# Attention's first near terms stored in two interleaved halves, later ones in two pieces

## The reference

```
x = x + 0.5 * L0_ffn(layernorm(x))          # switch MoE, 8 experts
x = x + L0_attn(layernorm(x))               # the part that is changed
x = x + 0.5 * L0_ffn(layernorm(x))
x = x + 0.5 * L1_ffn(layernorm(x))
x = x + L1_attn(layernorm(x))
x = x + 0.5 * L1_ffn(layernorm(x))
```

```
pos_k  = rel_embeddings @ Wk + bk                       # by head
scores = q k^T / scale
c2p    = take(q pos_k^T, clip(rel + 32, 0, 63))         # by (q, k)
p2c    = take(k pos_k^T, clip(-rel + 32, 0, 63))^T
probs  = softmax(scores + (c2p + p2c) / scale)
out    = layernorm((probs v) Wo + bo + hidden)
```

## Time and profile before

| | us |
|---|---|
| median of 3 runs | 788.8 (788.06 to 790.25) |
| the profiled execution | 788.52 |
| its span in the trace | 786.8 |
| attention's first instruction | 116.6 |
| the first `add_terms` | 180.16 |

### The profile page before, as it was taken

The page is one execution under the profiler, slowest core; times in us unless marked ns, Lnnn a source line. Parts: engine busy times, 40 slices in busy tenths (PEclk is TensorE's granted clock), DMA queues, the critical chain, the costliest instruction groups (busy, mean ns, idle before and its releaser), DMA issues. The chain is left out here.

```text
span 786.8 us, 16609 instructions
## 1 busy us (share of the span) xinstructions
PE 583.0 (74%) x5220; PEld 417.2 (53%) x5220; DVE 531.2 (68%) x1878; ACT 437.1 (56%) x944; POOL 219.6 (28%) x274
## 2 busy tenths in 40 slices
PE   4499927727999999999999998343993661686660
PEld 3387923324666566667666666233982451364460
DVE  7612235815787678989999995771226888766887
ACT  2034524415888788888888884631551523464522
POOL 1743422000950391095040000056442100212000
PEclk9999977866999999999999998655997655799655
DMA  8669525989989899999954413725552000000001
GB/s 251 179 182 391 185 79 169 289 342 269 283 274 335 220 278 348 324 225 271 338 157 129 124 48 99 165 76 146 180 166 71 0 1 1 0 1 2 0 1 53
DMA packets 133602, 130.79 MB, mean 166 GB/s; under 512 B 29565, under 2 KB 109485, under 8 KB 131853
## 3 DMA queue, kind: packets, MB, share of 16 engines
q1 hardware_dynamic: 126668, 103.61, 46.3%
q0 software_dynamic: 4736, 25.07, 8.7%
q10 hardware_dynamic: 2112, 1.05, 0.5%
HBM read 73.43 MB, written 52.92 MB: 161 GB/s over the span
## 5 line engine op out<-in xcount | busy, mean ns | idle before, releaser
L1442 DVE CUSTOM_DVE_ANT_0 l0am_prob<-l0am_ps_s,l0am_bias 128x512 f32<-128x512 f32 x256 | 161.6, 687 | 56.1 <-PE l0am_ps_s L1519 34.9
L1361 ACT ACTIVATE l0am_prob<-l0am_prob,l0am_neg_top 128x512 f32<-128x512 f32 x256 | 172.1, 730 | 19.1 <-DVE l0am_neg_top L1442 19.0
L1531 PE MATMUL l0am_ps_t<-c_ident,l0am_prob 128*128 128x128 f32 x1024 | 138.2, 279 | 0.0
L1531 PEld LDWEIGHTS l0am_ps_t<-c_ident,l0am_prob 128*128 128x128 f32 x1024 | 113.8, 142 | 16.7 <-issue 16.6
L1355 ACT COPY l0am_probT<-l0am_ps_t 128x512 f32<-128x512 f32 x128 | 69.0, 590 | 45.6 <-PE l0am_ps_t L1531 45.6
L1519 PE MATMUL l0am_ps_s<-l0am_ks,l0am_qs 32*128 32x512 f32 x512 | 74.0, 647 | 21.7 <-DVE l0am_neg_top L1442 19.5
L1429 DVE COPY l0am_probT<-l0am_ps_t 128x512 f32<-128x512 f32 x128 | 82.2, 683 | 2.5 <-PE l0am_ps_t L1531 2.4
L764 DVE COPY l0f_xsT<-l0f_psT 128x128 f32<-128x128 f32 x46 | 13.4, 292 | 97.5 <-PE l0f_psT L872 97.5
L593 ACT ACTIVATE l0f_h<-l0f_psU,l0f_experts 128x128 f32<-128x128 f32 x184 | 52.6, 368 | 47.2 <-PE l0f_psU L882 47.2
L1544 PE MATMUL l0am_ps_c<-l0am_probT,l0am_v 128*9 128x128 f32 x2048 | 67.9, 273 | 0.9 <-issue 0.9
L509 POOL DMA_INDIRECT token_results<-l0f_ys,l0f_token_i x46 | 44.3, 962 | 62.5 <-DVE l0f_ys L774 61.9
(11 more groups left out here) (312 smaller groups left out, 976.6 us busy)
## 6 DMA issues: line engine op xcount, KB each, us to landing
l0am_bias<-near_terms SPq DMA_DIRECT2D x128, 192.0 KB, 4.8
near_terms<-l0am_near POOLq DMA_DIRECT2D x12, 1536.0 KB, 8.3
l0f_mine<-l0f_experts SPq DMA_DIRECT2D x46, 256.0 KB, 2.8
l0am_rows_k<-position_k SPq DMA_DIRECT2D x16, 448.0 KB, 6.9
near_terms<-l0am_near SPq DMA_DIRECT2D x1, 6144.0 KB, 19.8
position_q<-l0am_rows SPq DMA_DIRECT2D x20, 224.0 KB, 4.8
position_k<-l0am_rows SPq DMA_DIRECT2D x20, 224.0 KB, 4.9
l0am_rows_q<-position_q SPq DMA_DIRECT2D x20, 224.0 KB, 6.0
```

What stands on the lines that cost most here:

```text
L1361: nc.scalar.activation(prob[:, k, :], prob[:, k, :], ACT.Exp, bias=neg_top[:, k:k + 1], scale=-1.0)\
L1442: dve.tensor_tensor_reduce(out=prob[:, k, :], in0=ps_s[:, j, :], in1=bias[:, j, at:at + S], scale=-1.0, scalar=HUGE, op0=ALU.add, op1=ALU.min,
L1531: last = pe.transpose(ps_t[:, u % 2, i, :], prob[:, u % SLOTS_, i * P:(i + 1) * P], ident[:, :])
```

## The change

There are five edits.

1. Batch 0's rows are laid out otherwise: heads 0 to 7 on the even partitions, heads 8 to 15 on the odd ones. Each of its row loads is issued as two DMAs, one a half (`half_view` steps two partitions at a time). Waits on `rows_in` count one batch more.
2. `store_first_near(half)` stores one half: 64 partitions, every second one. The even half holds groups 0 and 1. Bias loads of group 0 wait for it alone; the odd half is stored after them, and group 2's first bias load waits for it.
3. The first two row loads of batch 1 are issued between the first half's store and the wait for it; places 2 to 9 get new steps.
4. GpSimd stores the near terms of batches 1 to 3 in two DMAs of 32 queries each.
5. Batch 3's chunks are made at quads 15 to 26 (before: 13 to 24), and its row loads come at quads 24 to 33 (before: 21 to 30).

The diff, without two parts that only repeat what is listed (the k loads of batch 0, the same edit on TensorE):

```diff
@@ -116,7 +116,7 @@
 NEAR_AT = {0: 0, 3: 576, 1: 896, 2: 1344}
 BIAS_COLS = 1664
 FIRST_KEY = {t: NEAR_AT[t] - (2 * t - 1) * 64 for t in range(T4)}
-LATER_PIECES = tuple((q0, q0 + 16) for q0 in range(0, 64, 16))
+LATER_PIECES = ((0, 32), (32, 64))
 CHUNK_SPAN = CHUNK * S + MARGIN
 TAB_SPAN = MARGIN + TABLE_CHUNKS * CHUNK_SPAN
@@ -162,9 +162,9 @@
     steps = {}
-    for later, quads in ((1, [-1, -1, 0, 0, 1, 1, 2, 2, 3, 3]), (2, range(9, 19)), (3, range(21, 31))):
+    for later, first, quads in ((1, 2, [-4, -4, 0, 1, 1, 2, 2, 3]), (2, 0, range(9, 19)), (3, 0, range(24, 34))):
         for place, quad in enumerate(quads):
-            steps.setdefault(divmod(quad + T4, T4), []).append((later, place))
+            steps.setdefault(divmod(quad + T4, T4), []).append((later, first + place))
     return steps
@@ -1100,7 +1101,7 @@
         rows_out = [sem(f"rows_out{k}") for k in range(ROW_BUFS)]
         rows_in, far_out = [sem(f"rows_in{k}") for k in range(TABLE_CHUNKS)], sem("far_out")
         near_out = kept.enter_context(nc.semaphore(f"{name}_near_out"))
-        first_near_out = sem("first_near_out")
+        first_near_out = [sem(f"first_near_out{half}") for half in range(2)]
         near_steps, near_dve, near_pool = sem("near_steps"), sem("near_dve"), sem("near_pool")
         tiles_in = [sem(f"tiles_in{k}") for k in range(2)]
         bias_in = [sem(f"bias_in{t}") for t in range(T4)]
@@ -1124,16 +1125,23 @@
         def late_quad(cn):
-            return cn - EARLY + 1
+            return cn - EARLY + 1 if cn < LAST else cn - LAST + 15
+
+        late = {late_quad(cn): cn for cn in range(EARLY, B * BATCH_CHUNKS)}
         def view(what, offset, *dims):
             t = what[:, :].tensor
             return bass.AP(t, offset, [(t.shape[1], P), *dims])
+        def half_view(what, half, offset, *dims):
+
+            t = what[:, :].tensor
+            return bass.AP(t, half * t.shape[1] + offset, [(2 * t.shape[1], P // 2), *dims])
+
         def near_build(engine, b, between):
             def arrived(pair):
-                engine.wait_ge(rows_in[pair], 16 * PAIR_LOADS[pair] * (b + 1))
+                engine.wait_ge(rows_in[pair], 16 * PAIR_LOADS[pair] * (b + 2))
             arrived(0)
             arrived(1)
@@ -1176,6 +1184,12 @@
                 def load_q_rows(b, k, arrived):
                     r = k * ROWS_CHUNK
+                    if b == 0:
+                        for half in range(2):
+                            sp.dma_start(half_view(rows_q, half, r * 64, (64, ROWS_CHUNK), (1, 64)),
+                                         bass.AP(dram["tab"][0].tensor, row_address(b, r) + half * HEADS // 2 * S,
+                                                 [(64, P // 2), (HEADS * S, ROWS_CHUNK), (1, 64)])).then_inc(arrived, 16)
+                        return
                     sp.dma_start(view(rows_q, r * 64, (64, ROWS_CHUNK), (1, 64)),
                                  bass.AP(dram["tab"][0].tensor, row_address(b, r),
                                          [(64, P), (HEADS * S, ROWS_CHUNK), (1, 64)])).then_inc(arrived, 16)
...
@@ -1196,11 +1216,11 @@
                     wait_chunk(b * BATCH_CHUNKS + place)
                     (load_q_rows, load_k_rows)[side](b, CHUNK_ORDER[pair], rows_in[pair])
-                def store_first_near():
+                def store_first_near(half):
                     part = 64 * WIN
-                    own = [(part, P), (1, part)]
-                    sp.dma_start(bass.AP(dram["near"].tensor, 0, own), bass.AP(near[:, :].tensor, 0, own)).then_inc(first_near_out, 16)
+                    sp.dma_start(bass.AP(dram["near"].tensor, half * (P // 2) * part, [(part, P // 2), (1, part)]),
+                                 half_view(near, half, 0, (1, part))).then_inc(first_near_out[half], 16)
                 def store_far(b, part):
@@ -1244,11 +1264,14 @@
                         sp.wait_ge(far_out, 64)
                         load_tiles(0)
                 sp.wait_ge(near_dve, 1)
-                store_first_near()
+                store_first_near(0)
+                load_rows(1, 0)
+                load_rows(1, 1)
                 sp.wait_ge(filled, 1)
-                sp.wait_ge(first_near_out, 16)
+                sp.wait_ge(first_near_out[0], 16)
                 for t in range(T4):
                     load_bias(0, t)
+                store_first_near(1)
                 for cn in range(EARLY - ROW_BUFS, EARLY):
                     store_chunk(cn)
@@ -1266,12 +1289,13 @@
                         if n:
                             sp.wait_ge(neg_ready, 16 * (n - 1) + 4 * (t + 1))
-                            if g == 0 and t == 0:
+                            if n == GROUPS // 2 and t == 0:
+                                sp.wait_ge(first_near_out[1], 16)
+                            elif g == 0 and t == 0:
                                 sp.wait_ge(near_out, 16 * len(LATER_PIECES) * b)
                             load_bias(n, t)
-                        for cn in range(EARLY, B * BATCH_CHUNKS):
-                            if n and late_quad(cn) == 4 * (n - 1) + t:
-                                store_chunk(cn)
+                        if n and T4 * (n - 1) + t in late:
+                            store_chunk(late[T4 * (n - 1) + t])
                         for later, place in ROW_STEPS.get((n, t), ()):
                             if place == 0 and later > 1:
                                 sp.wait_ge(near_pool, later - 1)
@@ -1303,7 +1327,8 @@
                 for b in range(1, B):
                     if b == 1:
-                        pool.wait_ge(first_near_out, 16)
+                        for half in range(2):
+                            pool.wait_ge(first_near_out[half], 16)
                     near_build(pool, b, between).then_inc(near_pool, 1)
                     pool.wait_ge(near_pool, b)
                     for k, (q0, q1) in enumerate(LATER_PIECES):
@@ -1380,9 +1405,8 @@
                     if q < QUADS:
                         exp(4 * q + 2)
                         exp(4 * q + 3)
-                    cn = EARLY + q - 1
-                    if EARLY <= cn < B * BATCH_CHUNKS:
-                        copy_rows(cn, ps_g[:, :])
+                    if q in late:
+                        copy_rows(late[q], ps_g[:, :])
             @block.vector
             def _(dve):
...
```

More of the change, by code:

```diff
@@ L1074, in relative_attend @@
         EARLY = 2 * BATCH_CHUNKS
+        LAST = 3 * BATCH_CHUNKS
         stats, mv = sb("stats", [P, TILES, 6]), sb("mv", [P, TILES, 2])
@@ L1185, in load_k_rows @@
                     for n0, n1, start in NARROW_PIECES[k]:
+                        if b == 0:
+                            for half in range(2):
+                                sp.dma_start(half_view(rows_k, half, n0 * NARROW, (NARROW, n1 - n0), (1, NARROW)),
+                                             bass.AP(dram["tab"][1].tensor, row_address(b, n0) + start - 64 + half * HEADS // 2 * S,
+                                                     [(64, P // 2), (HEADS * S, n1 - n0), (1, NARROW)])).then_inc(arrived, 16)
+                            continue
                         sp.dma_start(view(rows_k, n0 * NARROW, (NARROW, n1 - n0), (1, NARROW)),
@@ L1556, in _ @@
                         score(q)
-                    cn = EARLY + q - 2
                     if 3 <= q:
-                        if EARLY <= cn < B * BATCH_CHUNKS:
-                            pe.wait_ge(rows_ready, cn + 1)
+                        if q - 1 in late:
+                            pe.wait_ge(rows_ready, late[q - 1] + 1)
                         turn_heads(q - 3)
@@ L1569, in _ @@
                         turn(4 * (q - 1) + 3)
-                    cn = EARLY + q - 1
-                    if EARLY <= cn < B * BATCH_CHUNKS:
-                        if cn == EARLY + 1:
-                            pe.wait_ge(rows_ready, cn)
+                    if q in late:
+                        if late[q] == EARLY + 1:
+                            pe.wait_ge(rows_ready, late[q])
                         if 3 <= q:
                             pe.wait_ge(heads_ready, q - 2)
-                        row_products(cn, ps_g[:, :])
+                        row_products(late[q], ps_g[:, :])
         clear_semaphores(nc, own_sems + aside.own_sems)
```

## The result

| | before | after |
|---|---|---|
| median, 20 runs each on one chip | 789.42 us | 786.58 us |
| ratio after / before, 95% interval | | 0.9962 (0.9945 to 0.9979) |
| profiled execution, its span | 788.52, 786.8 | 788.47, 786.8 |

The change gains 2.8 us by the medians, 1.7 to 4.3 by the interval. The forecast was 783, a gain of 5.6.

A forecast was written before the change was run, and what follows sets the result against it. The loop's head was taken to be bound by store, wait, load, with TensorE busy throughout the loop. Terms: -5.1 (first bias) + 2.5 (ScalarE) - 3.0 (slow quads) = -5.6, so 788.5 becomes 782.9, say 783; own range 779 to 787, whole range 779 to 798.

The forecast's parts named there:

- The half store: First near store before the loop: half the bytes at 446 GB/s takes 12.8 us instead of 19.8.
- Slow halves: Rival at the near store: 64-partition transfers run at 222 GB/s, a half takes 19.9 us, total 797; chance 0.32.
- The 12 extra issues: SyncE's queue ahead of the near store: splitting batch 0's row loads delays it 1.5 us, at most 5.2.
- The condition that the prediction had named: SyncE's queue before the loop: the prediction is wrong if it reaches the near store later than 159.
- Row loads ahead of the bias: Between first half's landing and add_terms: two batch 1 row loads before the bias loads add 0.5 us, bounds 0 and 2.6.
- ScalarE behind the second half: End of quad 1: ScalarE's copy of chunk 24 waits for chunk 20's store, 3.5 us late, 2.5 lost.
- GpSimd's first build near 190: Batch 1's near build in the loop: begins near 190 instead of 197.90, 8 us sooner.
- The slow quads: Loop at quad 16 and from 325.57 to 352.91: freed, 3.0 us gained, least 0, most 3.3.
- The second rival: Loop, quads 16 to 35: bias or tiles come late and the gain is given back, total 788; chance 0.15.
- The clock after attention: Layers after attention: the clock may shift a few us either way; with anything between, chance 0.05.

The follow-up runs named there:

- E2: Changed kernel with heads in old order, halves being partitions 0 to 63 and 64 to 127, batch 0's row loads single: 798.2 us, 1.0101 of before.
- E1: Kernel before with only batch 0's row loads each split into two DMAs over even and odd partitions: 792.2 us, 1.0037 of before.
- E4: Changed kernel with the odd half of batch 0's row loads issued by GpSimd on its own queue: 783.8 us, 0.9951 of before.
- E6: Changed kernel with GpSimd storing later batches' near terms in four pieces again: 787.2 us, 0.9996 of before.
- E7: Changed kernel with batch 3's chunks and row loads at the quads of before: 790.4 us, 1.0044 of before.
- E3: Changed kernel with the second half's store issued behind the stores of chunks 20 to 23: 784.8 us, 0.9938 of before.
- E10: Kernel before with only GpSimd's near stores of batches 1 to 3 in two pieces instead of four: 790.2 us, 1.0037 of before.
- E9: Kernel before with batch 0's row loads issued as 24 DMAs, each over 128 partitions and half of the rows: 789.1 us, 1.0029 of before.
- E12: Changed kernel with GpSimd issuing batch 0's odd-partition row loads and, on its own queue, the second half's store: 781.1 us, 0.9911 of before.

## Why the prediction was wrong

The direction held and the size did not: -2.8 measured, -5.6 forecast. Step by step, by the trace:

- **The half store: right.** 12.8 us forecast, 11.6 measured. "Slow halves" is refuted for interleaved partitions, at 423 GB/s while one is in flight; E2 shows it true for adjacent ones.
- **The 12 extra issues: wrong, and the step that failed.** 1.5 us was taken, between 0 and 5.2; it was 6.4. The price of 0.43 us is that of a load over 128 partitions; each half cost 0.65, so all 24 became dearer, not only 12 were added: 10.3 us more of issuing, not 5.2. The row with the right shape was at hand: eight bias loads over 64 partitions in 5.28 us, 0.66 each. The prediction let 3.7 of its 5.2 us be absorbed, and about as much was (3.9 of 10.3), but for another reason than it gave. "SyncE is held up by full rings that drain no slower for the split" was read out of one issue of 1.76 us, a chunk store's. Up to the last row load, 2.9 us went into SyncE's waits for chunks, and 1.4 came from stores that swell less. Then nothing was left: after, the engines were 83% busy and SyncE was the bound. E1 (the split alone delays the store as much) and E4 (half of the issues on another queue bring back 4.3 of 6.4) show it. The condition that the prediction had named, SyncE at the near store later than 159, came true: 164.89, or 162.1 without the 2.8 that the layer before took.
- **Row loads ahead of the bias, +0.5:** nothing to be seen; they are issued while the half is in flight, and bias issue to add_terms is 4.7 us, before 4.6.
- **ScalarE behind the second half: right.** 3.5 us late forecast, 3.31 measured; 2.5 lost forecast, 3.2 by the quads. E6 and E7, the same up to there, wait 3.05 and 3.48 us and lose 1.9 and 2.4. E3 shows that 1.75 us come back at quad 4 when only the order is changed.
- **GpSimd's first build near 190: wrong, at no cost.** It began at 200.15. The prediction let it hang on the second half's landing; it waited for batch 1's rows, whose k load of pair 1 held SyncE 5.46 us (at 187.44) behind the second half.
- **The slow quads, -3.0: about right in size (-3.7), in part by luck.** The reason given, two completions less, covers the change to batch 1 alone. Quads 30 to 35 are free in every kernel with edit 5, which the prediction had put at nothing; without it edit 4 moves the slow place to quad 27 and loses 8 us of loop.
- **Rivals.** The second rival let GpSimd's larger pieces make tiles late. In the changed kernel nothing of it is seen, but E7 and E10 show it at quad 27 (E10 near 41 too), with 8 us of loop, as soon as edit 5 is out. Its 788 lies nearer to the result than the forecast, for another reason. The clock after attention moved little: from the last VectorE copy of the loop to the end of the span it is 307.8 us before and 307.3 after.

With the split at 6.4 instead of 1.5 and the rest as forecast, the sum is -5.6 + 4.9 = -0.7; the half store (1.2 better) and the row loads (0.5) bring it to -2.4, and the loop's two terms (0.7 worse and 0.7 better) cancel; the trace has -2.2.

## What to carry to other kernels

A DMA that is split can cost its issuing queue more than the added issues at the old price: take the price from a row with the new shape, and multiply all of the issues by it, not only the added ones. If a timed store follows in the same queue, sum the queue up to that store, and take off what the issuing engine waits there now (here 10.3 us less about 4). An engine that has nothing to do can issue half of the loads. A large transfer that isn't urgent delays what is issued behind it, and to a lesser degree beside it, so list the next three things in the queue, not only the first.

## What the runs showed of the hardware

- A store of 3.15 MB in pieces of 49,152 bytes took 11.1 to 12.8 us from issue to landing over every second partition (11.4 in the trace of after) and 18.8 over 64 adjacent ones (E2); 6.3 MB over all 128 took 18.3 to 19.8 (E9 and before).
- SyncE's issue of a row load of batch 0 took 0.36 to 0.44 us over 128 partitions (before; one of 0.67, and 1.50 for three in a row), 0.49 to 0.60 over 128 with half of the rows, in a row of two or six (E9), and 0.58 to 0.70 over 64 partitions with all rows, also singly (E4). Stores of chunks between the loads over 64 partitions took 0.58 to 0.70 (one of 1.25), where they take 0.30 when the queue ahead is empty. Why a smaller load costs more to issue wasn't found.
- GpSimd issued the same half loads in 0.71 to 0.79 us each (E4), 0.63 in a row of three.
- With 3.15 MB in flight, a later issue of SyncE took 5.5 us (after, at 187.44), 8.3 (E7) and 5.9 (E12); in E7 and E12 the 3.15 MB were on GpSimd's queue.
